# Linear attention in quads of heads: fp32 scores in row groups, values in column groups

## The reference, cut to what matters

```
qkv = x @ Wqkv.T + bqkv                       # q, k, v split into 16 heads of D = 16
qp = relu(einsum('bhtd,hdm->bhtm', q_ch, proj))       # 64 features per head
kp = relu(einsum('bhtd,hdm->bhtm', k_ch, proj))
aw = einsum('bhtm,bhsm->bhts', qp, kp) * mask         # within a chunk of 128 tokens
out = (ctx_hist + einsum('bhts,bhsd->bhtd', aw, v_ch)) \
      / (norm_hist + aw.sum(-1) + DELTA)[..., None]   # history: running sums of kp and v
...
return out @ Wout.T + bout
x = _layernorm(x + _L1_attn_ref(x, ...))
x = _layernorm(x + _L1_xattn_ref(x, ctx_768, ...))    # softmax attention, 16 heads
x = _layernorm(x + _L1_ffn_ref(x, ...))
```

## Time and profile before

| what | us |
|---|---|
| median of 3 runs (lowest, highest) | 1669.56 (1666.37, 1675.34) |
| the profiled execution, its own time | 1684.5 |
| its span, first to last instruction | 1682.7 |
| PE busy, DVE busy, ACT busy, POOL busy | 1451.3, 1202.5, 622.5, 955.6 |

### The profile page before, as it was taken

How to read it: one execution, slowest core, us unless ns; L and a number is a source line. 1 busy time by engine, 2 the same in 40 slices (tenths; PEclk the granted TensorE clock), 3 DMA queues, 4 the chain that set the end, 5 groups by cost and what they waited for, 6 DMA issues and landing times.

```text
span 1682.7 us, 25828 instructions
## 1 busy us (share of the span) xinstructions
PE 1451.3 (86%) x9847; PEld 1264.4 (75%) x9847; DVE 1202.5 (71%) x2099; ACT 622.5 (37%) x1274; POOL 955.6 (57%) x975
## 2 busy tenths in 40 slices
PE   5777899899999999899999969888886199999990
PEld 5777678778778778799999957666664199999990
DVE  5889766766576586567766748877774387888886
ACT  3444211211111211155555524443342166666652
POOL 3324556556556656466676733555445378778762
PEclk9897899999999999999999969999996599999995
DMA  4100223223222222100000010000000266556624
GB/s 158 29 15 10 79 90 116 76 88 101 75 88 89 86 88 92 52 1 2 1 2 2 1 43 1 22 13 12 12 8 7 98 244 226 201 199 217 221 75 150
DMA packets 44985, 129.97 MB, mean 77 GB/s; under 512 B 8406, under 2 KB 23225, under 8 KB 38976
## 3 DMA queue, kind: packets, MB, share of 16 engines
q1 hardware_dynamic: 32688, 66.70, 12.2%
q0 software_dynamic: 12176, 61.63, 10.3%
HBM read 119.82 MB, written 10.31 MB: 77 GB/s over the span
## 4 chain that ended last, share of the span: by engine, by line
PE 63%; DVE 18%; issue 7%; POOL 5%; ACT 4%; DMA 2%; SPq 0%; another core or an unknown queue 0%; ACTq 0%; DVEq 0%; POOLq 0%
PE bank L425 15%; PE bank L426 14%; PE bank L427 14%; PE bank L1282 8%; PE bank L433 5%; PE bank L1036 4%; DVE hid_hi L1697 2%; DVE topE L1849 2%; PE bank L1169 2%; POOL slot_codes L720 2%; DVE hf L1716 1%; DVE shiftE L1856 1%; PE bank L1191 1%; ACT x_tok L471 1%; DVE cT L1585 1%
## 5 line engine op out<-in xcount | busy, mean ns | idle before, releaser
L1699 DVE TENSOR_TENSOR hid_lo<-hf,hid_hi 128x512 fp32r<-128x512 f32 x96 | 219.1, 2282 | 3.3
L561 POOL TENSOR_TENSOR wpiece_lo<-wraw,wpiece_hi 128x1024 fp32r<-128x1024 f32 x88 | 215.6, 2449 | 7.4
L425 PE MATMUL bank<-hid_hi,wpiece_lo 128*128 128x512 f32 x512 | 201.7, 394 | 8.4 <-DVE hid_lo L1699 8.4
L559 POOL TENSOR_SCALAR wpiece_hi<-wraw 128x1024 fp32r<-128x1024 f32 x88 | 93.8, 1066 | 196.8 <-PE bank L427 192.8
L426 PE MATMUL bank<-hid_lo,wpiece_hi 128*128 128x512 f32 x512 | 200.4, 391 | 0.0
L427 PE MATMUL bank<-hid_hi,wpiece_hi 128*128 128x512 f32 x512 | 200.3, 391 | 0.0
L1697 DVE CAST hid_hi<-hf 128x512 fp32r<-128x512 f32 x96 | 77.8, 810 | 125.9 <-ACT hf L1384 124.8
L674 POOL TENSOR_TENSOR aw_lo<-awm,aw_hi 128x384 fp32r<-128x384 f32 x128 | 127.8, 1020 | 47.8 <-ACT aw_hi L1444 47.6
L1384 ACT ACTIVATE hf<-bank,ffn_scales 128x512 f32<-128x512 f32 x64 | 44.1, 690 | 294.0 <-PE bank L427 294.0
L697 POOL TENSOR_SCALAR probE<-probE 128x1024 f32<-128x1024 f32 x64 | 66.4, 1039 | 118.0 <-ACT probE L1476 114.4
L425 PEld LDWEIGHTS bank<-hid_hi,wpiece_lo 128*128 128x128 f32 x512 | 96.8, 189 | 32.5 <-DVE hid_lo L1699 12.7
(11 more groups left out here) (360 smaller groups left out, 4633.7 us busy)
## 6 DMA issues: line engine op xcount, KB each, us to landing
wraw<-in_C_w SPq DMA_DIRECT2D x88, 512.0 KB, 3.3
yc<-y_rows SPq DMA_DIRECT2D x16, 256.0 KB, 5.9
ctx_raw<-in_ctxT SPq DMA_DIRECT2D x16, 192.0 KB
xraw<-in_xT SPq DMA_DIRECT2D x8, 256.0 KB, 3.9
x_tok<-in_x SPq DMA_DIRECT2D x8, 256.0 KB, 4.4
x_rows<-x_tok SPq DMA_DIRECT2D x8, 256.0 KB
out_x<-x_tok SPq DMA_DIRECT2D x8, 256.0 KB, 2.1
staging<-in_A_wqkv SPq DMA_DIRECT2D x1, 768.0 KB, 6.0
```

The source lines that it names most:

```text
L425: pe.e.matmul(o, sl, mh, start=start and i == 0, stop=False)
L559: pool.mark(pool.e.tensor_scalar(pair[0], raw, 1.0, 0.0, ALU.mult, ALU.add))
L561: pool.e.tensor_tensor(pair[1], raw, f(pair[0]), ALU.subtract).then_inc(done, 1)
L1699: dve.e.tensor_tensor(lo[:, o, :], hf[o % 2][:, :], f(hi[:, o, :]), ALU.subtract).then_inc(s_hid, 1)
```

## The change

**D works in quads.** `PAIR` becomes `QUAD`, four heads in four rounds (steps 0, 1 and 3 do something); four quads per batch. Nothing in a quad is split: `qkD`, `feat`, `aw` and `v_all` are fp32. Step 0: two fp32 matmuls of 32 rows by 128 columns and 512 moving columns (q and k side by side), one per pair, each in its own row group. ReLU by one ScalarE instruction of 1024 columns. Step 1: per pair four fp32 matmuls of 64 rows, the two heads in different halves of the rows; VectorE masks two heads in one instruction of 768 columns, straight to `aw`. Step 3: eight fp32 matmuls with 32 output columns, four heads in four column groups. `PLACE`, `v_heads`, `awm`, `csum` and all the `_hi`/`_lo` work of the quad are gone; `DR` and `values` are now shared by D and E.

**Banks.** Features take banks 0 and 1 together (`features`), scores banks 2 and 3 and banks 4 and 5 (`scores_d`, 1024 columns each), and everything else of D, so q, k, v, the sums, their transposes, and the three fills of `FIN`, takes turns on banks 6 and 7. Before D, TensorE waits until banks 0 to 5 are drained.

**Weights.** The loads of the cross-attention weights are issued in D, and GpSimd splits all four pairs in the round of the second batch's `PRE`; `v_all` is cleared before D.

```diff
-        base = 6 + PAIRS * b
-        items.append((base - 6, 0, "PRE", (b,), 3))
-        items += [(base + j, -(PAIRS * b + j), "PAIR", (b, j), 5) for j in range(PAIRS)]
+        base = 4 + QUADS * b
+        items.append((base - 4, 0, "PRE", (b,), 3))
+        items += [(base + i, 1, "QUAD", (b, i), 4) for i in range(QUADS)]
+        items += [(base + QUADS // KC * (c + 1) + 3, 0, "DR", (b, c), 1) for c in range(KC)]
         if b < B - 1:
+            items.append((base + QUADS + 4, 0, "FIN", (b,), 4))
...
+    features, scores_d, scores_e = range(8, 9), range(9, 11), range(8, 10)
...
+                    for k in range(2):
+                        pair = 2 * i + k
+                        rows = slice(32 * (pair % 4), 32 * (pair % 4) + 32)
+                        made = pe.e.matmul(u.ap[:, k * 512:(k + 1) * 512], proj[rows, pair, :], qk_d[b % 2][rows, pair // 4, :, :],
+                                           start=True, stop=True)
...
+                        for t in range(TT):
+                            for g in range(2):
+                                rows = slice(g * M, (g + 1) * M)
+                                o = u.ap[:, g * 512 + t * S:g * 512 + S + t * P]
+                                made = pe.e.matmul(o, ft[rows, k, 1, t * P:(t + 1) * P], ft[rows, k, 0, t * P:S], start=True, stop=True)
...
+                    for t in range(TT):
+                        for j in range(4):
+                            w = aw[(2 * (b * QUADS + i) + j // 2) % 8]
+                            made = pe.e.matmul(u.ap[32 * j:32 * j + 32, t * P:S], v_all[b % 2][:, t, 4 * i + j, :],
+                                               w[:, j % 2, t * S:S + t * P], start=t == 0, stop=t == TT - 1)
...
+            for i in range(6):
+                pe.wait_ge(drained[i], turns_before["D"][i])
...
-            pool.wait_ge(s_av, B * NH)
-            pool.wait_ge(l_stage[1], 80)
-            split([w[:, :, :] for w in ev], staged(1, a["E_wv"]), s_ev)
+                if name == "PRE" and step == 0 and args[0] == 1:
+                    pool.wait_ge(l_stage[0], 64)
+                    split([w[:, :, :] for w in dwo], staged(0, a["D_wo"]), s_dwo)
+                    for i, n, pair, src in ((1, 48, eq, "E_wq"), (1, 64, ek, "E_wk"), (0, 80, ev, "E_wv"), (1, 80, eo, "E_wo")):
+                        pool.wait_ge(l_stage[i], n)
+                        split([w[:, :, :] for w in pair], staged(i, a[src]), s_ew)
```

More of the change, by code:

```diff
@@ L44 @@
 PAIRS = NH // 2
+QUADS = NH // 4
 NPIECE = 2 * KC + 2 * FC + 2
@@ L170, in bank_order @@
         if name == "CN" and step == 1:
-            out.append((("C", "x", *args), low))
+            out.append((("C", "x", *args), held))
         elif name == "PRE":
[L173 to L182, removed]
+            out.append((("D", "qkv"[step], *args), held))
+        elif name == "QUAD" and step == 0:
+            out.append((("D", "f", *args), features))
+        elif name == "QUAD" and step == 1:
+            out += [(("D", "s", *args, k), scores_d) for k in range(2)]
+        elif name == "QUAD" and step == 3:
+            out.append((("D", "a", *args), held))
+        elif name == "DR":
+            out.append((("D", "t", *args), held))
         elif name == "FIN" and step in (0, 1, 3):
-            out.append((("D", "cox"[min(step, 2)], *args), low))
+            out.append((("D", "cox"[min(step, 2)], *args), held))
     for name, step, args in ES:
@@ L187, in bank_order @@
             out.append((("E", "qkv"[step - 1], *args), upper))
+        elif name == "PAIR" and step == 0:
+            out.append((("E", "s", *args), scores_e))
         elif name == "PAIR" and step == 2:
@@ L1056, in finish @@
                 if step == 0:
-                    made = use["E", "t", b, KC - 1]
-                    pe.wait_ge(*((s_ct, b * NAB + NAB) if stage == "D" else (made.drained, made.done)))
+                    last = use[stage, "t", b, KC - 1]
+                    pe.wait_ge(last.drained, last.done)
                     pe.wait_ge(uc.drained, uc.turn)
@@ L1196, in tensor_program @@
                 elif name == "DR":
-                    b, c = args
-                    u, last = use["E", "t", b, c], use["E", "a", b, 2 * c + 1]
-                    pe.wait_ge(last.drained, last.done)
-                    pe.wait_ge(u.drained, u.turn)
-                    into = u.ap[:, :].rearrange("p (t j two w) -> p t j two w", t=TT, j=4, two=2)
-                    transposes(pe, [(into[:, t, :, par, :], acc_e[c][:, par, t * P:(t + 1) * P])
-                                    for t in range(TT) for par in range(2)]).then_inc(u.filled, 1)
+                    drain_heads("E", *args)
                 elif name == "DFIN":
@@ L1232, in tensor_program @@
                         made.then_inc(u.filled, 1)
-            for p in range(PAIRS - 2, PAIRS):
-                last = use["E", "s", B - 1, p]
-                pe.wait_ge(last.drained, last.done)
+            for i in (8, 9):
+                pe.wait_ge(drained[i], turns_before["F"][i])
             u = use["F", "n"]
@@ new lines, in vector_program @@
+                elif name == "PRE" and step == 2:
+                    dve.wait_ge(l_db, 80)
+                    values("D", *args, dbv)
+                elif name == "QUAD" and step == 1:
+                    b, i = args
+                    for k in range(2):
+                        n, u = 2 * (b * QUADS + i) + k, use["D", "s", b, i, k]
+                        dve.wait_ge(u.filled, u.full)
+                        if n >= 8:
+                            old = use["D", "a", *divmod((n - 8) // 2, QUADS)]
+                            dve.wait_ge(old.filled, old.full)
+                        dve.e.tensor_tensor(aw[n % 8][:, :, :], u.ap[:, :].rearrange("p (g s) -> p g s", g=2)[:, :, 0:3 * P],
+                                            mask_d[:, None, :].to_broadcast([P, 2, 3 * P]), ALU.mult).then_inc(u.drained, 1)
+                elif name == "DR":
+                    drain_heads("D", *args)
```

393 lines of the change are left out of this document (122 added, 271 removed).

## The result

Measured beside each other, the changed kernel takes 1592.68 us (median of 4 runs, 1592.08 to 1597.01) and the kernel before 1672.45 (1666.37 to 1678.0): a ratio of 0.953, 95% interval 0.949 to 0.957. It is 80 us faster, and the prediction said 1548 within 1518 to 1590. The sign was right, and a third of the gain, 42 us of 122, is missing.

The account below looks back on a forecast made before the run. TensorE alone was taken to bound stage D at 32.15 us per batch. At 18.4 us per batch, the cross-attention's first scores would start at 872 instead of 993.66, so 1669.6 - 122 = 1548 us, range 1518 to 1590.

Parts of the forecast that it names:

- What bounds D: Stage D before the change: TensorE alone, busy 32.00 of 32 us at clock 1.00, a batch taking 32.15 us.
- TensorE's new matmuls: A quad in D: features 0.45, scores 0.65, values 0.33 and changes of kind 0.45, together 1.9 us on TensorE.
- The term for changes from kind to kind: In each quad on TensorE: three changes at about 0.1 to 0.2 us each, 0.45 us together.
- the three parts of the distance that hold quads: In D: rounds 4 to 11 take 24 us, five full batches 92, the last full set of quads 13.
- the 0.3 for a lower clock: In a batch of D: gaps on TensorE lower the clock now and then, adding 0.3 us.
- The other engines' sums: Per batch of D after the change: VectorE 13.6 us, ScalarE 10, GpSimd about 2.
- What is late next: Banks 6 and 7 in D: TensorE's stalls waiting for drains total 2.5 us per batch, a period of 18.1.
- Entry and exit: Into D: v of batch 0 done at about 719 us; out to the cross-attention: about 12 us against 23.8 before.
- From profile to median: Whole kernel: the profiled execution lay 14.9 us over the median; the same difference was taken off, giving 1548.
- Clock stays low: Rival: low clock through D gives 1618 us, for half of D 1583; chance 0.10 for half or more.
- Groups don't overlap: Rival: D's fp32 matmuls run one after the other, 3.5 instead of 1.4 us per quad, 1595; chance 0.09.
- Slower: Rival: D's fp32 matmuls run one by one at twice the time per column, 1708 us; chance 0.03.

Follow-up runs that it names:

- a3: Changed kernel with both feature matmuls of a quad reading the same rows, hence one row group; 1643.05 us (one run), ratio 0.970 to the kernel before.
- a1: Changed kernel with operands of features and scores rounded to fp32r, one pass each, low part left out; 1564.94 us, ratio 0.923 to the kernel before.
- c1: Changed kernel with only the scores in one pass of fp32r; 1568.30 us, ratio 0.938 to the kernel before.
- c2: Changed kernel with only the features in one pass of fp32r; 1576.70 us, ratio 0.941 to the kernel before.
- b1: Changed kernel with the item that transposes and divides the sums put first in its round; 1585.90 us, ratio 0.947 to the kernel before.
- a5: Changed kernel with the cross-attention's weights loaded and split late, as before the change; 1599.16 us, ratio 0.956 to the kernel before.
- b2: Changed kernel with the edits of a1 and b1 together; 1549.39 us, ratio 0.925 to the kernel before.
- b3: b2 with the cross-attention's scores in one pass of fp32r too; 1549.84 us, ratio 0.925 to the kernel before.
- a4: Changed kernel with a pair's scores ordered by head, then key tile; 1610.16 us (one run), ratio 0.951 to the kernel before.

## Why the prediction was right or wrong

**What bounds D** was right, before and after: TensorE, at a granted clock of 1.00.

**TensorE's new matmuls** is the step that failed, with its sentence "inside a run I take 0.22 to 0.25 us for 256 fp32 columns, whatever stands side by side". It divided the time of a run by the count of trace rows. The count of matmuls, which the order of the program gives, is half of it (the loops in the diff say so too: two, eight and eight per quad; the trace has four, sixteen and sixteen). Start to start the rows of one fp32 matmul are 0.216 us apart for 256 columns (scores) and 0.43 for 512 (a3), and there are two of them: 0.43 for 256 columns, which at 2.4 GHz is four clock periods per column. That makes features 0.85 instead of 0.45 (measured 1.06 with the start of the run), scores 1.28 instead of 0.65 (1.51), values 0.64 instead of 0.33 (0.79). The term for changes from kind to kind was 0.45; what lies over the pure columns is 0.15 to 0.23 in each kind, together 0.6, so it was a little small.

The Trainium skill has this price, in "FP8 and Floating Point Precision", section "TensorE Precision Notes": true fp32 takes four passes through the array. By that rule the trace agrees to the digit: 256 columns four times at 2.4 GHz are 0.427 us, and the trace has twice 0.216. Weighed against my rows ahead of the run it would have shown the miscount, since 0.22 to 0.25 is two passes.

In the sum: the three parts of the distance that hold quads are too long by 27.5, 9.1 and 6.3 us, 42.9 of the 43.1 us between predicted and measured distance. The price alone would give more, 1.5 us for each of four quads and so 6.0 per batch instead of 5.5; against it, the stalls were 2.1 and not 2.5, and the 0.3 for a lower clock did not come. a1, c1 and c2 show the price: with two instructions for one taken away, the period goes below the predicted 18.4, and by the expected amount for each kind. Only the values were in no run made in one pass, so their share, 0.46 of the 1.5 us, is read from rows and not tested.

**The other engines' sums** were right: 952 ns for a mask (0.95), 1026 for a ReLU (1.02), 424 for half a `ctxtok` (0.42), 692 for a `_lo` (0.69).

**What is late next** was right in kind and size. The prediction had 1.6, 0.4 and 0.5 us of stall per batch ahead of the sums, behind `xt_lo`, `ctxT_lo` and k; the trace has 1.31, 0.33 and 0.49. A longer quad did not cover them, as one might think: in these rounds TensorE waits with its quad already done. But the pair of banks is no law: b1 shows that another order inside a round takes 1.35 us off the period, and TensorE then stands for 0.9 us of a batch instead of 2.1.

**Entry and exit.** The first quad at 718.9, for "about 719"; the exit 11.6, for 12. No wait of TensorE in D is put down to GpSimd's splits. The comparison with before was wrong, though. It set 12, counted from `ctxtok`, against 23.8, counted from the start of the last values' matmuls. Counted from those, the changed kernel needs 16.7 us (898.26 to 914.96) and a5 22.8 (898.23 to 921.04). So the passage became 7.1 us shorter by this count, of which the early weights give 6.1, and not 12. The forecast was not hurt by it, since the sum took only the 12 of the changed kernel.

**From profile to median.** The profiled execution of before lay 14.9 us over the median, and I took off the same. That came out right: the changed kernel's profile has no such excess, and the first scores and the medians moved by the same amount. Behind the first scores the profile of before is 13.8 us longer. Where that lies is only in part to be seen: the profile of before has idle time with no releaser ahead of one group of products in the routed block, most of which the changed kernel's hasn't got (before, after). No other profile of before shows whether its other runs have it.

```profile
L1282 PE MATMUL bank<-w_hi,gh_lo 128*128 128x256 f32 x368 | 105.9, 288 | 16.5 <-issue 14.9
```

```profile
L1212 PE MATMUL bank<-w_hi,gh_lo 128*128 128x256 f32 x368 | 106.0, 288 | 5.7 <-DVE gh_lo L1887 2.2
```

So the profiles differ by 92 us, the medians by 80, and the first scores by 79.

**The rivals.** *Clock stays low:* not in the changed kernel (1.00 in every stretch from 738 to 866 us). So what the Trainium skill tells of cycling PSUM banks ("TensorE: Matmul & The Clock Gate", section "A second HAM failure mode: psum-queue depth-cycling") does not show in its D, though TensorE has short idle times in every batch. In b2 and in a3, whose D uses the same two banks, the clock falls for two batches. TensorE of a3 is busy for 28.9 of 31 us there, so its idle share alone does not explain it; what brings the lower clock on stays open. *Groups don't overlap:* the time came out near this rival's 1595, but a3 shows for features that it is not its mechanism, and the scores start in twos 6 ns apart. A forecast can be hit for the wrong reason, and here it would have been. *Slower:* its price of fp32 matmuls, twice the time per column, was the true one, and its other half, one by one, false; the two together were 0.03. Taken apart they would have been worth a rival of their own, "right overlap, double price": a quad is 2.86 + 0.45 = 3.3, 7.6 becomes 13.2, and the batch 18.4 + 5.6 = 24.0, which is what happened.

## What to carry to other kernels

Before dividing a run's time by the rows of a trace, count the operations in the code that they stand for, and see that two independent counts agree; a factor of two there goes straight into the sum. When a rival is a product of two conditions, give each condition its own case. And where several items share a pair of buffers, try which drain precedes which fill: one number in a table gave 0.5% here, and moving the wrong item gave nothing.

A version beats both kernels at once: a1, with 0.923 of the time of before (b2 and b3 are level with it). It pays with the low part of features and scores. At full fp32 it is b1, at 0.947.

## What the runs showed of the hardware

An fp32 matmul is two instructions, which together take four clock periods per column at 2.4 GHz: on 32 rows 0.43 us per instruction of 512 columns (a3), on 64 and on 128 rows 0.216 per instruction of 256 (scores and values). Only a transpose of fp32 data is one instruction, 128 columns in 0.109 us.

fp32r gained nothing from row groups on 32 rows. Twelve split matmuls of 256 columns on 128 rows start 0.12 us apart. In a1 two matmuls of 512 columns in two row groups start 3 ns apart and take 0.43 us together, and b3's scores of 256 columns come in twos every 0.22 us: just what the same columns would need one after the other at one clock period per column. The starts speak for two at once at half the speed, but no run puts fp32r matmuls on one row group, as a3 does with fp32, so this is not shown. On 64 rows it is different: in a1's scores a pair of 128 columns starts 0.06 us ahead of the next pair, and a pair of 256 columns 0.17.

fp32 matmuls in different halves of the rows overlap almost as well when the program lists them one half after the other (a4: 0.1 us more per 16 instructions).
